# A fused graph-attention, expert, latent-attention and quantized-FFN kernel: the first integers of the FFN spread over the attention before it, and one softmax shift in four moved to ScalarE

## The reference, cut to what matters

```
x: (4, 256, 256)   ctx: (4, 256, 64)
# graph attention, 8 heads of 32, two layers, per graph
e     = leaky_relu(attn_self[:, :, None] + attn_neigh[:, None, :], 0.2) - 1e10 * (1 - adj)
alpha = softmax(e, -1);  out = elu(alpha @ feat + b)          # adj = layernorm(x)
x = x + out
x = x + experts(layernorm(x)) + shared(layernorm(x))          # 16 experts, top 4
# latent attention, 16 heads
x = x + softmax(q_r @ k_r.T) @ ctx_c ... @ Wo                 # q from layernorm(x)
# quantized FFN, hidden 704
def quant(x): s = 127 / max(|x|) ; return clip(round(x * s), -128, 127) / s
x13 = quant(layernorm(x)) @ w13.T;  gated = relu(x1)**2 * x3
x = x + quant(rmsnorm(gated) * norm_w) @ w2.T
```

## Time and profile before

| what | value |
|---|---|
| median of 3 runs | 555.82 us (555.39 to 558.62) |
| the profiled execution | 556.21 us, of it span 554.4 us |
| mean granted TensorE clock | 0.957 of full speed |
| busy: PE, DVE, ACT, POOL | 477.1, 354.7, 270.9, 152.7 us |
| chain that ended last | PE 61%, DVE 20%, ACT 6%, issue 6%, POOL 5% |

### The profile page before, as it was taken

The page is one execution under the profiler, slowest core; times in us unless marked ns, Lnnn a source line. Parts: engine busy times, 40 slices in busy tenths (PEclk is TensorE's granted clock), DMA queues, the critical chain, the costliest instruction groups (busy, mean ns, idle before and its releaser), DMA issues.

```text
span 554.4 us, 9661 instructions
## 1 busy us (share of the span) xinstructions
PE 477.1 (86%) x3268; PEld 317.1 (57%) x3268; DVE 354.7 (64%) x1103; ACT 270.9 (49%) x678; POOL 152.7 (28%) x225
## 2 busy tenths in 40 slices
PE   3797899998686999998986899899999956798896
PEld 2464566665454545773564576676676734475553
DVE  4798999999748931233773755656555487357662
ACT  2486788886453313332124465465356244145661
POOL 0000000001150006705478344234333243022340
PEclk9998999998997999999997899999999999699996
DMA  8990000000150405972238000000000000000000
GB/s 212 328 201 6 1 2 1 4 1 2 29 130 1 175 10 152 285 208 86 59 93 88 9 1 2 1 1 1 1 2 2 0 1 1 1 1 9 21 19 30
DMA packets 28370, 30.15 MB, mean 54 GB/s; under 512 B 4673, under 2 KB 26402, under 8 KB 28066
## 3 DMA queue, kind: packets, MB, share of 16 engines
q1 hardware_dynamic: 25554, 24.74, 15.8%
q0 software_dynamic: 1536, 4.20, 4.4%
q10 hardware_dynamic: 1232, 0.60, 0.4%
HBM read 26.38 MB, written 3.15 MB: 53 GB/s over the span
## 4 chain that ended last, share of the span: by engine, by line
PE 61%; DVE 20%; ACT 6%; issue 6%; POOL 5%; DMA 1%; ACTq 0%; DVEq 0%
PE bank L872 5%; PE bank L768 5%; PE bank L862 5%; PE bank L850 4%; PE bank L823 4%; POOL arena L1852 4%; PE bank L782 3%; PE bank L584 3%; PE bank L935 3%; PE bank L838 3%; DVE work L1396 3%; PE bank L595 3%; PE bank L968 3%; ACT work L1203 3%; PE bank L604 2%
## 5 line engine op out<-in xcount | busy, mean ns | idle before, releaser
L1203 ACT ACTIVATE work<-bank,nmx 128x256 f32<-128x256 f32 x128 | 58.8, 472 | 61.2 <-DVE nmx L1647 61.1
L1863 POOL TENSOR_SCALAR work<-work,R 128x256 f32<-128x256 f32 x128 | 61.4, 495 | 65.8 <-DVE R L1659 65.8
L1396 DVE CUSTOM_DVE_ANT_0 work<-bank,Nw 128x256 f32<-128x256 f32 x128 | 46.5, 420 | 9.2 <-PE bank L570 9.1
L862 PE MATMUL bank<-halves,kvb 128*64 128x256 f32 x256 | 38.0, 418 | 15.3 <-DVE halves L1638 15.3
L1647 DVE TENSOR_REDUCE nmx<-bank 128x2 f32<-128x512 f32 x64 | 41.2, 684 | 12.0 <-PE bank L850 11.7
L850 PE MATMUL bank<-work 64*128 64x256 f32 x256 | 44.2, 419 | 3.2 <-ACT work L1203 3.0
L1852 POOL DMA_INDIRECT arena<-eout,idx x32 | 31.7, 991 | 30.8 <-DMA eout<-work 21.5
L1056 ACT ACTIVATE bank<-bank 128x512 f32<-128x512 f32 x64 | 34.9, 595 | 9.5 <-PE bank L570 9.5
L838 PE MATMUL bank<-ident,work 128*128 128x128 f32 x256 | 36.1, 287 | 4.0 <-POOL work L1863 4.0
L1796 POOL TENSOR_TENSOR rstd<-veps,half 128x2 f32<-128x2 f32 x12 | 8.9, 742 | 102.5 <-DVE veps L1325 102.5
L1063 ACT ACTIVATE work<-bank 128x512 f32<-128x512 f32 x64 | 35.0, 601 | 3.4 <-PE bank L584 3.4
(11 more groups left out here) (218 smaller groups left out, 929.4 us busy)
## 6 DMA issues: line engine op xcount, KB each, us to landing
work<-in_wg SPq DMA_DIRECT2D x16, 176.0 KB, 3.6
work<-in_wu SPq DMA_DIRECT2D x16, 176.0 KB, 4.3
work<-in_wd SPq DMA_DIRECT2D x16, 176.0 KB
arena<-in_wq SPq DMA_DIRECT2D x1, 2048.0 KB, 9.8
arena<-in_woT SPq DMA_DIRECT2D x1, 2048.0 KB, 16.4
eout<-work SPq DMA_DIRECT2D x16, 128.0 KB, 3.4
arena<-in_kcqT SPq DMA_DIRECT2D x1, 1536.0 KB, 21.6
arena<-in_w13T SPq DMA_DIRECT2D x1, 1408.0 KB, 8.2
```

The source lines that it names most:

```text
L862: mm = pe.matmul(bank[4 + j % 2][h * CD:(h + 1) * CD, 0:S], kvb[:, m, :], ET2[:, j % 2, h, m, :], start=m == 0, stop=m == 1, tile_position ...
L1203: act.activation(E2[:, j % 2, t, h, :], bank[h][:, t * S:(t + 1) * S], ACT.Exp, bias=nmx[:, j % 2, h, t:t + 1], accum_out=S2[:, j % 2, h, ...
L1396: dve.tensor_tensor_reduce(L[:, i % 4, t, :], bank[XB[i % 4]][:, t * S:(t + 1) * S], maskN[:, g, t, :], 1.0, -3.4e38, ALU.add, ALU.max, M[ ...
L1863: pool.tensor_scalar(E2[:, j % 2, t, h, :], E2[:, j % 2, t, h, :], R2[:, j % 2, h, t:t + 1], 1.0, ALU.mult, ALU.mult).then_inc(en2_ready, 1)
```

## The change

Three things move, and one is new.

1. `ff_first` and its statistics. Statistics of batch 0 and 1 go to b = 2, j = 4 and 7, after the reciprocal; `ff_first` 0 and 1 to b = 2, j = 5 and 6; 2 and 3 behind the reciprocals of pairs 0 and 1 of batch 3 (still in the turn b = 2). In b = 3 only statistics of batch 2 (j = 2) and `ff_first` 4 and 5 (j = 8 and 9) are left. 6 and 7 go from n = 0, 1 to n = 2, 4 of the FFN loop, and `ff_in_transposes`/`ff_in_evac` of tiles 4, 5, 6, 7 go to n = 0, 1, 2, 4. `ff_first` writes to a new buffer `centred` instead of `xln`. POOL's `ff_root` moves along.
2. On ACT `ff_back_evac(6)` goes from turn 6 to turn 5, ahead of `ff_square(7)`.
3. In graph attention the shift of the heads with i % 4 == 3 (the second head of each odd step: 16 of 64) leaves DVE. ACT does it in `below_largest`, as Identity with scale -1 and the largest as bias; the exponential of these heads then has scale -1.

```diff
             def score_transposes(i):
-                pe.wait_ge(d_ready, 2 * i + 2)
+                if i % 4 < 3:
+                    pe.wait_ge(d_ready, 2 * (i // 4 * 3 + i % 4 + 1))
+                else:
+                    pe.wait_ge(n_ready, 2 * (i // 4 + 1))
...
             def ff_back_transposes(n):
-                pe.wait_ge(f_q1T, min(n + 5, NT))
+                pe.wait_ge(f_q1T, (4, 5, 6, 7, 7, 8, 8, 8)[n])
...
-                if n + 5 < NT:
-                    ff_in_transposes(n + 5, n + 1)
+                if n in (0, 1, 2, 4):
+                    ff_in_transposes((4, 5, 6, None, 7)[n], n + 1)
...
+            def below_largest(i):
+                for t in range(TB):
+                    act.wait_ge(masked, 2 * i + t + 1)
+                    act.activation(L[:, i % 4, t, :], L[:, i % 4, t, :], ACT.Identity, scale=-1.0,
+                                   bias=M[:, i % 4, t:t + 1]).then_inc(n_ready, 1)
...
+                if s % 2 == 1 and 0 <= s < PAIRS:
+                    below_largest(2 * s + 1)
...
             for n in range(-2, NT):
-                if n >= 0:
+                if 0 <= n and n != NT - 2:
                     ff_back_evac(n)
                 if n + 2 < NT:
                     ff_relu(n + 2)
                 if 0 <= n + 1 < NT:
                     ff_integers(n + 1)
+                if n == NT - 3:
+                    ff_back_evac(n + 1)
                 if n + 2 < NT:
                     ff_square(n + 2)
-                if n >= 0 and n + 5 < NT:
-                    ff_in_evac(n + 5)
+                if n in (0, 1, 2, 4):
+                    ff_in_evac((4, 5, 6, None, 7)[n])
...
                     shift(2 * s)
-                    shift(2 * s + 1)
+                    if s % 2 == 0:
+                        shift(2 * s + 1)
...
                     att_inverse(b, j)
+                    if b == B - 2 and j in (4, 7):
+                        i = (j - 4) // 3
+                        layernorm_stats(i, base, f_veps, keep_at=i)
+                    if b == B - 2 and j in (5, 6):
+                        ff_first(j - 5, base)
...
                     att_inverse(b + 1, j)
+                    if b == B - 2:
+                        ff_first(j + 2, base)
...
-                if j in (2, 3, 4):
-                    layernorm_stats(j - 2, base, f_veps, keep_at=j - 2)
+                if j == 2:
+                    layernorm_stats(2, base, f_veps, keep_at=2)
-                if 3 <= j <= 8:
-                    ff_first(j - 3, base)
+                if j >= AH // 2:
+                    ff_first(j - 4, base)
...
-                if n in (0, 1):
-                    ff_first(6 + n, base)
+                if n in (2, 4):
+                    ff_first(5 + n // 2, base)
```

More of the change, by code:

```diff
@@ L237, in build @@
         tmp1 = piece([D])
+        centred = piece([D])
         q2T = piece([2, 6 * P], BF16)
@@ L297, in build @@
         d_ready = sem("d_ready")
+        n_ready = sem("n_ready")
         dT_done = sem("dT_done")
@@ L994, in _ @@
                 att_context(B - 1, j - 2)
-                if j >= 5:
+                if 5 <= j <= 8:
                     ff_in_transposes(j - 5, 0)
@@ L1062, in exponentials @@
                     act.wait_ge(agg_mm, q - 1)
-                act.activation(ET[:, q % 2, i % 4, :], bank[2 + i % 2][:, :], ACT.Exp).then_inc(e_done, 1)
+                act.activation(ET[:, q % 2, i % 4, :], bank[2 + i % 2][:, :], ACT.Exp,
+                               scale=-1.0 if i % 4 == 3 else 1.0).then_inc(e_done, 1)
+            def below_largest(i):
[3 more added lines that the diff above has]
+                                   bias=M[:, i % 4, t:t + 1]).then_inc(n_ready, 1)
             def agg_copy(q):
@@ L1674, in ff_first @@
                 dve.wait_ge(f_rstd, b + 1)
-                link(dve.tensor_scalar(xln[:, t, :], row(b, t), fstat[:, b, 2 * t:2 * t + 1], fstat[:, b, 4 + t:5 + t],
+                link(dve.tensor_scalar(centred[:, :], row(b, t), fstat[:, b, 2 * t:2 * t + 1], fstat[:, b, 4 + t:5 + t],
                                        ALU.subtract, ALU.mult), base)
-                link(dve.tensor_reduce(amax1[:, n:n + 1], xln[:, t, :], AX_X, ALU.max,
+                link(dve.tensor_reduce(amax1[:, n:n + 1], centred[:, :], AX_X, ALU.max,
                                        apply_absolute_value=True), base)
@@ L1680, in ff_first @@
                 link(dve.reciprocal(scl1[:, n:n + 1], is1[:, n:n + 1]), base)
-                link(to_integers(tmp1[:, :], xln[:, t, :], scl1[:, n:n + 1], base), base)
+                link(to_integers(tmp1[:, :], centred[:, :], scl1[:, n:n + 1], base), base)
                 dve.tensor_scalar(q1[:, n, :], tmp1[:, :], ROUND, None, ALU.subtract).then_inc(f_q1, 1)
@@ L1865, in normalise, with ff_root @@
                                            ALU.mult).then_inc(en2_ready, 1)
+            def ff_root(b):
+                root(b + 1, f_veps, f_rstd, fveps[:, b, :], fstat[:, b, 4:6])
             normalise(0, 0)
@@ L1871, in _ @@
                 for j in range(2, AH // 2):
+                    if b == B - 2 and j == 5:
+                        ff_root(0)
                     normalise(b, j)
+                if b == B - 2:
+                    ff_root(1)
                 for j in range(2):
                     normalise(b + 1, j)
-            def ff_root(b):
-                root(b + 1, f_veps, f_rstd, fveps[:, b, :], fstat[:, b, 4:6])
             for j in range(2, AH // 2):
-                if j in (2, 3, 4):
-                    ff_root(j - 2)
+                if j == 3:
+                    ff_root(2)
                 normalise(B - 1, j)
```

## The result

The changed kernel takes 551.79 us (median of 7 runs, 547.87 to 553.35), the kernel before 557.33 us (7 runs, 555.34 to 558.62): a ratio of 0.9905, 95% interval 0.9883 to 0.9927. So it is faster, by 4.1 to 6.5 us, but the forecast of 546.6 us was too low by 5.2.

What follows compares the result with a forecast made beforehand. It took TensorE as bound in mid graph attention and VectorE in the last batch's steps. Terms -9.9 - 4.0 - 0.7 + 4.8 + 2.0 - 1.4 = -9.2 from 556.2 gave 547.0, less 0.4: 546.6 us; range 542.3 to 552.5.

Steps and rivals of the forecast that it cites:

- last batch, pairs 3 to 7: Latent attention, batch 3: four steps without `ff_first` at 3.65 us, 14.6 us instead of 24.54, so -9.9 us.
- pair 7 to the first product: End of the last batch: last maximum to first FFN product in 9.65 us instead of 13.69, so -4.0 us.
- batch 2 and the two steps behind: Latent attention: added `ff_first` costs +1.08 in two steps and +2.35 in one, statistics and queries +0.3; sum +4.8 us.
- FFN loop and end: FFN loop: turns 0 and 1 -4.2, turn 2 +1.7, turn 4 +3.9, early ScalarE copy +0.6; together +2.0 us.
- graph attention: Graph attention: moved shifts save VectorE 2.3 us, ScalarE's new work costs 0.5 and its queueing 0.4; -1.4 us.
- rival of long steps: Last batch: steps without `ff_first` held at 4.88 us, -5.0 instead of -9.9, total 551.5 us; chance 0.11.
- The next one: Batch 3, `ff_first` of tile 3: hidden by the 32 matmuls of `att_output`; 2.5 us if that cover were gone.
- bound of -3: Pair 7 to first FFN product: gain of only 3 us, as TensorE waits about 2.4 us and its clock may fall.
- FFN pays more: FFN loop: new waits at turns 2 and 4 lower the clock and last longer, +5 not +2; 549.6 us, chance 0.13.
- clock kept: Graph attention: shorter waits for masks could keep the clock, worth at most 2.4 us; total 544.2 us, chance 0.17.
- ScalarE's cost: Graph attention: 32 new ScalarE instructions exceed idle time by 0.12 us a turn, +0.5 in four turns (0 to +2.2).
- the queue at s = 11: Graph attention: copy of hidden rows, exponentials, folds and `agg_copy` queue up on ScalarE once, +0.45 us.

Runs made afterwards that it cites:

- after_again: The changed kernel run again unaltered, for more rounds and a second profile; 551.28 us, 0.9882 of the kernel before.
- tile2_later: The changed kernel with `ff_first(2)` moved behind the last copy of the batch, where `att_output` hides it; 541.92 us, 0.9707 of the kernel before.
- pe_kept_busy: The changed kernel with TensorE transposing the identity, unread, in its waits; 543.49 us, 0.9735 of the kernel before.
- combined: The changed kernel with `ff_first(2)` behind the batch's last copy and FFN tiles 5 to 7 fed as before the change; 539.00 us, 0.9662 of before.
- tile2_later_again: Repeat of `tile2_later`, as partner of `combined` on the same chip; 544.64 us, 0.9753 of the kernel before.
- integers_only: The changed kernel without point 3, all shifts back on VectorE; 555.05 us, 0.9939 of the kernel before.
- graph_only: The kernel before with point 3 of the change alone, the moved shifts; 553.43 us, 0.9921 of the kernel before.
- back_evac_late: The changed kernel with point 2 taken back, `ff_back_evac(6)` in turn 6 again; 551.83 us, 0.9883 of the kernel before.

## Why the prediction was right or wrong

Term by term, against before; "measured" are the differences of the table, with the second profile of after behind the comma where it differs. For graph attention it is the sum of the places named below, without the clock near 50 us.

| term | predicted | measured |
|---|---|---|
| last batch, pairs 3 to 7 | -9.9 | -9.99 |
| pair 7 to the first product | -4.0 | -3.11, -3.25 |
| clock of the first product | -0.7 | -0.58, -0.41 |
| batch 2 and the two steps behind | +4.8 | +7.32, +7.54 |
| FFN loop and end | +2.0 | +3.33, +3.42 |
| graph attention | -1.4 | -4.1 |
| sum | -9.2 | -7.1, -6.8 |

*Last batch: right.* Without `ff_first` the ring of maximum, exponentials and scores gives 3.64 us a step. The rival of long steps fell.

*Batch 2: the step that failed.* The steps came out as worked out: +0.08, +1.07, +1.08, +0.40 and +2.36 us, 4.99 in all, against 4.8. But "The next one ... is hidden by the 32 matmuls" was true of tile 3 alone. I had priced what `ff_first(2)` costs on VectorE and stopped at the next maximum. I did not ask how long TensorE stands for the copy that this chain holds back: 2.28 us, in front of 40 matmuls. They ran at the lower clock for +2.33 us (+2.52 in `after_again`), which the sum had at nothing; `tile2_later` and `pe_kept_busy` show it by getting all of it back.

*Hand-over: the chain right, its clock not.* The context of pair 7 began 8.26 us after the last maximum (I had about 8.5), but took 1.98 us and not 1.0. The bound of -3, "its clock may fall again", was the case, in both profiles of after. It does not follow from the wait alone: `combined`, `tile2_later` and `tile2_later_again` kept 1.09 us behind the same one, though in `tile2_later` the clock fell a little later (19.52 us from the first FFN product to `ff_out(0)`, 17.99 in the other two).

*FFN loop: the waits right, their consequence mis-sized.* Turns 0 and 1 gave -4.1 (forecast -4.2), turn 2 +1.61 (+1.7), turn 5 +0.33 (+0.6). Turn 4 took 11.87 us, +5.56 instead of +3.9: its waits of 1.64 and 1.88 us are those forecast, and the 1.69 us on top are the product of tile 7 at the lower clock. With TensorE kept busy the turn took 10.18 us, the forecast's 6.3 + 3.9. This was the rival "FFN pays more", at 0.13; I had argued against it from a single wait of 2.25 us at 506.94 that had kept its clock.

*Graph attention: too little.* VectorE's relief at s = 5, 9, 25 and 29 was right, 0.52 to 0.53 us each for the 0.57 worked out. Two more places gave the same again. One is s = 1: mask 1 to 2 took 7.37 us before and 7.36 in `integers_only`, 6.85 in after and 6.84 in `after_again`. The other is s = 27: `integers_only`, which like `graph_only` keeps its clock there, takes 7.27 us from mask 27 to mask 29 and `graph_only` 6.74. Before took 7.67: there the clock fell behind the wait of the earlier trace rows, and 0.4 us of the gain is that. The rival "clock kept" was right about at 126, at a sixth of its price. ScalarE's cost was the wrong sign: no turn became longer, three became 0.17 to 0.23 shorter, and the queue at s = 11, for which I had +0.4, does not show (turn 9 to 13 is shorter by 0.52, all of VectorE's relief). Six times 0.53, 0.57 in the three turns and the 0.4 of the clock are the 4.1. Mask 1 to 31 confirms it: 118.59 us in `integers_only` and 114.90 in after, both without a fall of the clock near 50 us, are 3.7 apart, and the clock's 0.4 comes on top.

One instruction of the new kind costs 0.40 us of ScalarE in a row, by the timeline of after: two start at 85.79 and the next thing at 86.59.

```profile
85.79 0.92 ACT L1075 ACTIVATE work<-work,M 128x256 f32<-128x256 f32 x2
86.59 1.10 ACT L1068 ACTIVATE work<-bank 128x512 f32<-128x512 f32 x2
```

I had taken 0.43, from rows of the same shape but other operands. The Trainium skill, ScalarE: Activation LUTs, section "What ACT_TABLE_LOAD costs", gave an estimate of 0.40 us and with it 1.60 us in a turn, just the idle time; the trace agrees with the price. In a turn ScalarE's busy time rose by 1.31 us (12.70 to 14.01) and not by 1.60, its idle time before was 1.70, and 0.2 us a turn are left.

*What remains of the miss.* The terms were 2.1 to 2.4 us too hopeful (-9.2 against -7.1 and -6.8): batch 2, the hand-over and the FFN loop together by 4.7 to 4.9, while graph attention was too cautious by 2.7. Another 1.5 is the reference: the median of before was 555.82 us in three runs and 557.33 in seven, so part of the 5.2 is not a matter of the change. About 1.5 us is left, less than what stretches outside the change differ by between two executions.

## What to carry to other kernels

When work is moved ahead on a feeding engine, price two things: the feeder's own step, and the longest wait that this puts in front of a long run of matmuls, for behind such a wait (2.2 to 2.3 us here, or two of 1.6 and 1.9) the matmuls themselves took up to 1.8 times as long, though not in every execution. Put such work behind the last hand-over to TensorE and in front of its longest uninterrupted run, as `ff_first` behind the copy that `att_output` needs: the chain of tile 2 cost 4.7 us ahead of that copy (2.36 of its own, 2.33 of clock) and nothing behind it. And before one engine is filled up to relieve another, find the floor of the stretch: here it was TensorE's 13.9 us a turn by its busy time, and a second helping of ScalarE work took the whole gain back.

## What the runs showed of the hardware that was not expected

The clock after a wait is not settled by the length of the wait. After the same wait of 2.2 us for the last copy, the context took 1.98 us in after, 1.85 in `after_again`, 1.51 in `back_evac_late` and 1.09 in `tile2_later` and `combined`. Even in one kernel it differs: before kept 1.09 us behind waits of 2.34 and 2.28 us in the last batch and took 1.98 behind 2.64 and 3.77, while `graph_only`, alike there, took 1.96 behind 2.34. In `back_evac_late` the context behind the wait ahead of `att_output` (2.29 us) still took 1.09, but `att_output` behind it took 8.86, so the fall comes some time after the wait. What decides it stays open.

Execution to execution, the same stages differ in a few fixed places: 22.6 or 24.1 us from the router's logits to the experts' first product, in kernels that are alike there (22.60 before, 24.20 in `after_again`, 22.57 in `back_evac_late`), and 12.9 to 16.3 us at the end. Single runs of one kernel spread over 2 to 8 us, so it is the stage times that tell apart what is smaller.

In graph attention TensorE's busy time in a turn fell with its feeders' load, from 14.10 to 13.91 us at equal instructions and clock 1.00, and to 13.89 without ScalarE's part; with ScalarE's part doubled it is 14.21. Ends of matmuls are modelled in the profile, so this may be waiting inside a group that is shown as busy; no run here tells.
